# A graph network on one core: TensorE works on the row fetch one chunk further ahead, with the buffers still double

## The chip, the cores and the metric

The kernel runs on one core of a Trainium2 chip. The metric is device time in microseconds, measured without a profiler: the kernel before takes 26865.84 us (median of 3 runs, 26846.94 to 26884.09). A profiled execution of the same program takes longer, and this matters here.

## The reference

Four graph layers follow one another over the same graph of 12,500 nodes and 412,500 directed edges (source `src`, destination `dst`, sorted by destination). Each layer normalises `x`, keeps its positive part `h`, and adds the layer's result to `x`. Per edge a message is made from the source node's row `h[src]`, and the messages of one destination are summed:

```
layer 0: msg = h[src] * edge_weight * weight                      (one number per edge)
layer 1: msg = silu(h[src] x edge_attr_8 x W_msg_tp) @ W_msg_lin  (a tensor product)
layer 2: msg = (h[src] @ W_rel[edge_type]) * e                    (a matrix per relation)
layer 3: w = kernel_net(edge_attr_6), a 16x16 matrix per edge;
         four times: h = gelu(mean over edges of h[src] @ w + h @ root_W + root_b)
out = segment_sum(msg, dst)
```

## The kernel before, in words

Six passes run over the edges in the function `edge_pass`: "weighted" (layer 0), "relational" (layer 2), "kernel_net" (first step of layer 3, which also stores the edge matrices) and three times "kernel_kept" (the other steps, which load them again). Layer 1 has a pass of its own, which is not touched. Partition p holds a stretch of the sorted edges. A pass is a loop over `CHUNKS` = 202 chunks of 16 edges per partition, each edge being one column `j`; even chunks use buffer half b = 0 and odd ones b = 1.

Source rows come in two ways. For columns 0 to 11 (all 16 in kernel_net) GpSimd issues one indirect DMA per column (`gather_chunk`, L575) into `got`, a ring of 4 chunks, so GpSimd may be up to four chunks ahead of VectorE; a buffer comes free with `got_used`. The last X = 4 columns of the five passes other than kernel_net are fetched with matmuls, in these steps for each chunk:

- `hot_rows`: a one-hot of each edge's place in the table, 13 tiles in `place_hot`. ScalarE makes tiles 0 to 8 (nine `near` at L940, then one `place_hot` at L945), VectorE tiles 9 to 12 (L1004).
- place sums (`in_place_sums`, L777): 37 matmuls of 128x512 in four quarters (9, 9, 9 and 10), from `place_hot` and the table's three bf16 parts `tparts`, into `in_place`.
- `pick` on VectorE (L1011): keeps in `picked` the table range that holds the row.
- row sums (`in_row_sums`, L786): four small float32 matmuls with `fold` into `in_row`.
- `fetch` on VectorE (L1019): copies `in_row` into `got` beside the gathered rows.

VectorE then makes the message. In the relational pass a chunk has four groups g; TensorE makes a group's matrices in `wmat` (12 matmuls, L830, two buffers), VectorE multiplies (`product`, L1070) and reduces (`reduce`, L1078). The matrices of group g wait in `matrices` for the product two groups before, that is for a free buffer. A scan (L1111) sums within a destination, ScalarE copies the result (L930) and SyncE stores it. In SyncE's `load` stand the loads of indices, places (`place_b`) and ranges (`range_b`), one chunk after another in order.

The order on each engine is written by hand; semaphores alone tie the engines. Before, TensorE in chunk k makes the row sums of k, three quarters of the place sums of k + 1, and the first quarter of k + 2, which waits for `fetch` of k.

Of the kernel before, what the change touches and what calls it, by code (L numbers as in the profile page):

```python
# [29 lines left out]
P = 128  # L30
# [5 lines left out]
C = 16  # L36
# [543 lines left out]
def edge_pass(nc, a, SB, kind, table):  # L580
# [15 lines left out]
    with ExitStack() as ctx:  # L596
# [56 lines left out]
        with phase(nc, *names) as (block, *sems):  # L653
# [9 lines left out]
            def _(sp):  # L663
# [16 lines left out]
                def load(k, r, q, at):  # L680
# [21 lines left out]
                    if X:  # L702

                        sp.wait_ge(S["hot_by_act"], k + 1)
                        sp.wait_ge(S["hot_by_dve"], k + 1)
                        load_places(k + 2, b)

                        if not (first and b == 0):
                            sp.wait_ge(S["picked_made"], k)
                        load_ranges(k + 1, 1 - b)  # L710
# [27 lines left out]
                if X:  # L738
                    load_places(0, 0)
                    load_places(1, 1)  # L740
                    load_ranges(0, 0)
                    load_whole()
                rounds(sp, load)
# [23 lines left out]
            def _(pe):  # L767
                def in_place_sums(k, b, q, first=False):
# [3 lines left out]
                    if q == 0 and not first:  # L772
                        pe.wait_ge(S["fetched"], k - 1)
# [25 lines left out]
                def close_sums():  # L799

                    for h in range(XH):
                        pe.matmul(in_place[1][:, h, :], SB["zero_b"][:, 0:P], SB["zero_b"][:, 0:XC], start=False, stop=True)

                if X:
                    pe.wait_ge(S["parts_made"], 1)
                    for q in range(4):
                        in_place_sums(0, 0, q, first=True)
                    in_place_sums(1, 1, 0, first=True)

                if kind == "weighted":  # L810

                    pe.matmul(hist[:, :], SB["zero_b"][:, 0:P], SB["zero_b"][:, 0:NQ], start=True, stop=False, skip_group_check=True)
                    with pe.Fori(0, TURNS) as i:
                        for b in range(HALVES):
                            for g in range(4):
                                around(i * HALVES + b, b, g)
                            pe.wait_ge(S["hot_made"], i * HALVES + b + 1)
                            for j in range(C):
                                mm = pe.matmul(hist[:, :], ohp[:, b, j, :], ohq[:, b, j, :], start=False, stop=False, skip_group_check=True)
                            mm.then_inc(S["hot_used"], 1)  # L820
                    close_sums()
# [12 lines left out]
                if kind == "relational":  # L834
                    with pe.Fori(0, TURNS) as i:
                        for b in range(HALVES):
                            pe.wait_ge(S["hot_made"], i * HALVES + b + 1)
                            for g in range(GROUPS):
                                matrices(i * HALVES * GROUPS + b * GROUPS + g, g % 2, onehot[:, b, g * GE:(g + 1) * GE],
                                         [SB["wrel"][:, m, :] for m in range(PIECES)])  # L840
                                around(i * HALVES + b, b, g)
                    close_sums()
                    return

                if kind == "kernel_kept":
                    with pe.Fori(0, TURNS) as i:
                        for b in range(HALVES):
                            for g in range(GROUPS):
                                around(i * HALVES + b, b, g)
                    close_sums()  # L850
# [33 lines left out]
            def _(act):  # L884
# [61 lines left out]

                for b in range(HALVES):
                    hot_rows(b, b, 0, True)
                spread_mask(0, 0, True)
                for b in range(HALVES):  # L950
                    spread_mask(b + 1, 1 - b, b == 0)
                    hot_rows(b + 2, b, 1)
                    turn_out(b, b, 0, True)
                with act.Fori(1, TURNS - 1) as i:
                    for b in range(HALVES):
                        spread_mask(i * HALVES + b + 1, 1 - b, False)
                        hot_rows(i * HALVES + b + 2, b, i + 1)
                        turn_out(i * HALVES + b, b, i, False)
                spread_mask(CHUNKS - 1, 1, False)
                hot_rows(CHUNKS, 0, TURNS)  # L960
                turn_out(CHUNKS - 2, 0, TURNS - 1, False)
                hot_rows(CHUNKS + 1, 1, TURNS)
                turn_out(CHUNKS - 1, 1, TURNS - 1, False)
# [4 lines left out]
            def _(dve):  # L968
# [38 lines left out]
                def pick(k, b, turn_no):  # L1007

                    dve.wait_ge(S["in_place_made"], k + 1)
                    dve.wait_ge(range_in[b], turn_no * 16 + 16)  # L1010
                    dve.scalar_tensor_tensor(out=picked[:, :].rearrange("p (h e) -> p h e", h=XH),  # L1011
# [10 lines left out]
                def chunk(k, r, q, at):  # L1022
# [3 lines left out]
                    rows_v = got[:, r, :].rearrange("p (j f) -> p j f", f=W)  # L1026

# [1212 lines left out]
```

## Time and profile before

| what | value |
|---|---|
| time, median of 3 runs | 26865.84 us |
| span of the profiled execution | 31834.1 us |
| busy share of that span: TensorE, VectorE, ScalarE, GpSimd | 66%, 61%, 40%, 63% |
| mean granted TensorE clock, share of 2.4 GHz | 0.781 |

The span runs from the first to the last instruction of the one profiled execution. Its own time as the runs are timed isn't given; the span alone is 4968 us above the median of the runs. So the profile has idle time that the timed runs don't have, and the busy shares above are shares of the longer span.

### The profile page before, as it was taken

The page shows a single profiled execution, that of the slowest core. Times are in us where ns is not written, and L with a number is a line of the kernel's source. Part 1 is how long each engine was busy: PE and PEld are TensorE (multiplying, and loading weights), DVE is VectorE, ACT ScalarE, POOL GpSimd, SP SyncE. Part 2 cuts the span into 40 slices and gives each one's busy share as a digit, 9 for nine tenths or more (in the row PEclk, how much of TensorE's full clock was granted, in tenths as well). Part 3 has the DMA queues.
Part 4 walks back from the last instruction along what each step waited for, and adds up shares of the span by engine and source line. Part 5 has one row for each costly group of instructions (what it writes and reads, how often), then busy time and mean ns, then how long its engine had stood idle before and what let it go on. Part 6 is the DMA issues. An engine that isn't in the chain of part 4 may idle for free. (4 is left out here: it accounts for less than half of the span.)

```text
span 31834.1 us, 357740 instructions
## 1 busy us (share of the span) xinstructions
PE 21003.5 (66%) x95045; PEld 10976.5 (34%) x95045; DVE 19470.8 (61%) x31805; ACT 12595.6 (40%) x14673; POOL 20017.5 (63%) x18077
## 2 busy tenths in 40 slices
PE   4666649999867777756666666566655656465654
PEld 2333326666533333323333333222222222222222
DVE  4444448888756666645555555566665766566665
ACT  4555511111134444431111111455555655455554
POOL 4666657777734444445555555677776777766666
PEclk8777769999877777777777777777777777777777
DMA  1111125555412222212222222444444544444443
GB/s 38 34 33 34 34 59 93 92 92 93 89 42 50 50 49 49 49 44 86 84 86 84 85 84 82 120 138 146 143 127 130 147 140 145 113 136 136 140 135 106
DMA packets 2202951, 2877.61 MB, mean 90 GB/s; under 512 B 962293, under 2 KB 1687075, under 8 KB 2175143
## 3 DMA queue, kind: packets, MB, share of 16 engines
q1 hardware_dynamic: 1369250, 2680.20, 26.7%
q0 software_dynamic: 804512, 169.87, 8.0%
q10 hardware_dynamic: 29088, 26.49, 0.2%
q8 instruction: 29, 0.48, 0.0%
q14 instruction: 72, 0.58, 0.0%
HBM read 2203.20 MB, written 671.60 MB: 90 GB/s over the span
## 5 line engine op out<-in xcount | busy, mean ns | idle before, releaser
L575 POOL DMA_INDIRECT got<-table,idx x15352 | 16035.5, 1045 | 10224.3 <-issue 4522.0
L777 PE MATMUL in_place<-place_hot,tparts 128*128 128x512 bf16 x37600 | 10862.7, 441 | 5734.9 <-issue 2698.7
L777 PEld LDWEIGHTS in_place<-place_hot,tparts 128*128 128x128 bf16 x37600 | 4005.5, 111 | 11806.1 <-issue 7382.3
L940 ACT ACTIVATE near<-place_b,far_lanes 128x512 bf16<-128x512 f16 x9180 | 5713.3, 707 | 61.9 <-DMA place_b<-place_row 61.4
L1078 DVE TENSOR_REDUCE msg<-prod 128x64 f32<-128x1024 f32 x4040 | 4904.5, 1214 | 103.3
L945 ACT ACTIVATE place_hot<-near,one 128x4608 bf16<-128x4608 bf16 x1020 | 4218.3, 4136 | 1004.0 <-remote 810.9
L930 ACT ACTIVATE outb<-run 128x256 f32<-128x256 f32 (+1 forms) x1010 | 739.3, 732 | 8309.1 <-DVEq L1115 6614.4
L1492 POOL DMA_INDIRECT added<-rows,add_idx x2020 | 3318.9, 1643 | 962.2 <-issue 866.7
L1070 DVE TENSOR_TENSOR prod<-w_in,got 128x1024 f32<-128x1024 f32 x2424 | 2909.9, 1220 | 303.7 <-DMA got<-table,idx 176.5
L1535 PE MATMUL acc<-hot,spread 128*128 128x392 bf16 x14544 | 2849.5, 353 | 0.0
L1063 DVE TENSOR_TENSOR wcopy<-wmat,b 128x1024 f32<-128x1024 f32 x808 | 988.3, 1223 | 2445.7 <-remote 2050.1
L1019 DVE COPY got<-in_row 128x64 f32<-128x64 f32 (+1 forms) x1010 | 227.8, 226 | 3214.3 <-remote 3130.4
L830 PE MATMUL wmat<-k,h 128*128 128x256 f32 x6464 | 1928.1, 452 | 392.4 <-ACT h L896 254.4
L865 PE MATMUL h2p<-h,k 128*128 128x512 f32 x1616 | 1091.7, 763 | 1471.1 <-ACT h L890 1237.2
L890 ACT ACTIVATE h<-h1p,b 128x512 f32<-128x512 f32 x808 | 555.0, 687 | 3713.3 <-remote 2189.7
L1070 DVE TENSOR_TENSOR prod<-wmat,got 128x1024 f32<-128x1024 f32 x808 | 980.6, 1223 | 1652.5 <-remote 1288.9
L830 PEld LDWEIGHTS wmat<-k,h 128*128 128x128 f32 x6464 | 1461.8, 231 | 1171.1 <-issue 499.2
L1011 DVE SCALAR_TENSOR_TENSOR picked<-range_b,range_col,in_place 128x512 f32<-128x512 f16 x1015 | 758.3, 747 | 1803.9 <-remote 1274.0
L1535 PEld LDWEIGHTS acc<-hot,spread 128*128 128x128 bf16 x14544 | 1498.8, 106 | 1020.1 <-issue 258.2
L830 PE MATMUL wmat<-wrel,onehot 90*128 90x256 bf16 x9696 | 1542.9, 305 | 393.6 <-issue 375.3
L786 PE MATMUL in_row<-fold,picked 128*128 128x16 f32 x6464 | 862.0, 266 | 1304.6 <-DVE picked L1011 793.1
L786 PEld LDWEIGHTS in_row<-fold,picked 128*128 128x128 f32 x6464 | 891.3, 204 | 1507.3 <-DVE picked L1011 855.1
(253 smaller groups left out, 18740.6 us busy)
## 6 DMA issues: line engine op xcount, KB each, us to landing
w_in<-kept SPq DMA_DIRECT2D x2424, 512.0 KB
kept<-wcopy SPq DMA_DIRECT2D x808, 512.0 KB
got<-table,idx POOLq DMA_INDIRECT x15352
attr<-in_edge_attr SPq DMA_DIRECT2D x202, 1024.0 KB
place_b<-place_row SPq DMA_DIRECT2D x1020, 128.0 KB
range_b<-range_row SPq DMA_DIRECT2D x1015, 128.0 KB
sums<-outb SPq DMA_DIRECT2D x1010, 128.0 KB
rows<-in_src_row SPq DMA_DIRECT2D x202, 640.0 KB
```

The source lines that it names most:

```text
L575: pool.indirect_dma_start(out=dst[:, j * width:(j + 1) * width], out_offset=None, in_=table, in_offset=bass.IndirectOffsetOnAxis(ap=idx[:, ...
L777: mm = pe.matmul(in_place[b][:, h, :], tparts[:, s, t, :], place_hot[:, b, t, h * XC:(h + 1) * XC], start=(t == 0 and s == 0), stop=(t == ...
L786: mm = pe.matmul(in_row[b][:, j * FW:(j + 1) * FW], picked[:, j * P:(j + 1) * P], fold[:, :], start=True, stop=True)
L830: mm = pe.matmul(wmat[s2][:, j * DD:(j + 1) * DD], weights[:, j * P:(j + 1) * P], moving, start=(m == 0), stop=(m == len(moving_parts) - 1))
L865: pe.matmul(h2p[n % 2][:, :], SB["k2"][:, :], h1[:, n % 2, :], start=True, stop=True).then_inc(S["h2_made"], 1)
L940: act.activation(near[:, t, :], place_b[:, b, :], ACT.Abs, bias=SB["far_lanes"][:, t:t + 1]).then_inc(S["near_made"], 1)
L945: act.activation(place_hot[:, b, 0:ACT_HOTS, :], near[:, :, :], ACT.Relu, bias=SB["one"][:, 0:1], scale=-1.0).then_inc(S["hot_by_act"], 1)
L1063: dve.tensor_tensor(wcopy[:, g, :].rearrange("p (j d) -> p j d", j=G), wmat[g % 2][:, :].rearrange("p (j d) -> p j d", j=G), bcast(SB["b3" ...
L1070: dve.tensor_tensor(prod[:, g % 2, :].rearrange("p (j o i) -> p j o i", j=G, o=D), w.rearrange("p (j o i) -> p j o i", j=G, o=D), bcast(ro ...
L1078: c.step(dve.tensor_reduce(msg[:, b, 0:D, g * G:(g + 1) * G].rearrange("p o j -> p j o"), prod[:, g % 2, :].rearrange("p (j o i) -> p j o ...
L1492: pool.indirect_dma_start(out=SB["added"][y], out_offset=bass.IndirectOffsetOnAxis(ap=add_idx[:, b, y:y + 1], axis=0), in_=add_rows[:, b, ...
L1535: mm = pe.matmul(acc[c][:, 0:RCOLS], spread[:, b, j, s, :], hot[:, b, j, c * RCOLS:(c + 1) * RCOLS], start=False, stop=False, skip_group_c ...
```

## The change

In the five passes with X = 4 each step of the fetch stands one chunk earlier against the rest: in chunk k ScalarE and VectorE make the one-hots of k + 3 (before: k + 2), TensorE all four quarters of the place sums of k + 2 and the row sums of k + 1 (before: of k), and VectorE picks k + 1 at the start of chunk k (before: at the end of it). `place_hot`, `in_place` and `in_row` stay double, `picked` single. Place sums wait for `picked_made` where they waited for `fetched`; row sums also wait for `fetched`, and `pick` for `in_row_made`. At the head of a pass TensorE makes the place sums of chunks 0 and 1 in full; at its end nothing is made for chunks that don't exist. kernel_net is unchanged.

```diff
                     if q == 0 and not first:
-                        pe.wait_ge(S["fetched"], k - 1)
+                        pe.wait_ge(S["picked_made"], k - 1)
...
                     pe.wait_ge(S["picked_made"], k + 1)
+
+                    pe.wait_ge(S["fetched"], k)
...
-                def around(k, b, g):
-
-
-                    if g == 1:
-                        in_row_sums(k, b)
-                    if g < 3:
-                        in_place_sums(k + 1, 1 - b, g + 1)
-                    else:
-                        in_place_sums(k + 2, b, 0)
+                def around(k, b, g, at=None):
+
+                    if g == 2 and (at is None or at + 1 < CHUNKS):
+                        in_row_sums(k + 1, 1 - b)
+                    if at is None or at + 2 < CHUNKS:
+                        in_place_sums(k + 2, b, g)
...
                 if X:
                     pe.wait_ge(S["parts_made"], 1)
-                    for q in range(4):
-                        in_place_sums(0, 0, q, first=True)
-                    in_place_sums(1, 1, 0, first=True)
+                    for b in range(HALVES):
+                        for q in range(4):
+                            in_place_sums(b, b, q, first=True)
+                    in_row_sums(0, 0)
...
+                def turn(k, b, i, at):
+                    if at is None or at + 1 < CHUNKS:
+                        spread_mask(k + 1, 1 - b, at == 0)
+                    if at is None or at + 3 < CHUNKS:
+                        hot_rows(k + 3, 1 - b, i + 1 + b)
+                    turn_out(k, b, i, at is not None and at < HALVES)
...
+                    if X and (at is None or at + 1 < CHUNKS):
+
+                        pick(k + 1, 1 - b, i + b)
+                    if X and (at is None or at + 3 < CHUNKS):
+                        hot_rows(k + 3, 1 - b, i + 1 + b)
...
-                    if X:
-
-                        pick(k + 1, 1 - b, i + b)
```

SyncE's `load` follows: in chunk k it loads the places of k + 3 (after the one-hots of k + 1) and the ranges of k + 2 (after the pick of k).

TensorE in the relational pass, before: the prologue and the first chunk of the loop (half 0). `in_place_7512` is half 0, `in_place_7513` half 1.

```order
1091 L777 MATMUL in_place_7512<-place_hot,tparts 128x512 x37
1092 L777 MATMUL in_place_7513<-place_hot,tparts 128x512 x9
1096 L830 MATMUL wmat_7517<-wrel,onehot 128x256 x12
1098 L777 MATMUL in_place_7513<-place_hot,tparts 128x512 x9
1100 L830 MATMUL wmat_7518<-wrel,onehot 128x256 x12
1101 L786 MATMUL in_row_7514<-fold_rel,picked 128x17 x4
1102 L777 MATMUL in_place_7513<-place_hot,tparts 128x512 x9
1104 L830 MATMUL wmat_7517<-wrel,onehot 128x256 x12
1105 L777 MATMUL in_place_7513<-place_hot,tparts 128x512 x10
1107 L830 MATMUL wmat_7518<-wrel,onehot 128x256 x12
1109 L777 MATMUL in_place_7512<-place_hot,tparts 128x512 x9
```

The same place in the changed kernel, where `in_place_7589` is half 0 and `in_place_7590` half 1.

```order
1091 L780 MATMUL in_place_7589<-place_hot,tparts 128x512 x37
1092 L780 MATMUL in_place_7590<-place_hot,tparts 128x512 x37
1093 L791 MATMUL in_row_7591<-fold_rel,picked 128x17 x4
1097 L837 MATMUL wmat_7594<-wrel,onehot 128x256 x12
1099 L780 MATMUL in_place_7589<-place_hot,tparts 128x512 x9
1101 L837 MATMUL wmat_7595<-wrel,onehot 128x256 x12
1102 L780 MATMUL in_place_7589<-place_hot,tparts 128x512 x9
1104 L837 MATMUL wmat_7594<-wrel,onehot 128x256 x12
1106 L791 MATMUL in_row_7592<-fold_rel,picked 128x17 x4
1107 L780 MATMUL in_place_7589<-place_hot,tparts 128x512 x9
1109 L837 MATMUL wmat_7595<-wrel,onehot 128x256 x12
1110 L780 MATMUL in_place_7589<-place_hot,tparts 128x512 x10
```

The prologue has 28 place sums more and the first row sums; in the chunk, the row sums moved from behind the matrices of g = 1 to behind those of g = 2, so that row sums and nine place sums stand between the matrices of g = 2 and of g = 3 where ten place sums stood.

VectorE at the turn from one relational chunk to the next, before:

```order
1292 L1078 TENSOR_REDUCE msg<-prod 128x4x16
1293 L1097 TENSOR_TENSOR msg<-msg,emix 128x256
1295 L1111 SCALAR_TENSOR_TENSOR run<-mask,msg 128x512
1296 L1011 SCALAR_TENSOR_TENSOR picked<-range_b,range_col,in_place_7513 128x512
1297 L1004 TENSOR_SCALAR place_hot<-place_b,lanes 128x512 x4
1298 L1046 TENSOR_TENSOR eprod<-attr,wvec 128x256
```

And in the changed kernel:

```order
1293 L1091 TENSOR_REDUCE msg<-prod 128x4x16
1294 L1110 TENSOR_TENSOR msg<-msg,emix 128x256
1296 L1124 SCALAR_TENSOR_TENSOR run<-mask,msg 128x512
1297 L1022 SCALAR_TENSOR_TENSOR picked<-range_b,range_col,in_place_7589 128x512
1298 L1012 TENSOR_SCALAR place_hot<-place_b,lanes 128x512 x4
1299 L1059 TENSOR_TENSOR eprod<-attr,wvec 128x256
```

The instructions and their order are the same; pick and one-hots are those of one chunk later, as the other buffer half in the pick's row shows.

## Rows read from the trace of the kernel before

**Rows 1.** The page, its first line.

```profile
span 31834.1 us, 357740 instructions
```

**Rows 2.** Groups on GpSimd, one pass each (weighted, kernel_net, first kernel_kept): count, busy, mean.

```profile
L575 POOL DMA_INDIRECT got<-table,idx x2424 | 2366.2, 976 | 1668.2 <-DVEq L1035 814.1 <-issue 678.0 <-DMA idx<-in_src 176.1
L575 POOL DMA_INDIRECT got<-table,idx x3232 | 3220.5, 996 | 2546.5 <-DVEq L1099 1389.6 <-issue 972.8 <-DMA idx<-in_src 184.1
L575 POOL DMA_INDIRECT got<-table,idx x2424 | 2720.6, 1122 | 954.6 <-issue 732.9 <-DVEq L1099 195.1 <-DMA idx<-in_src 26.5
```

**Rows 3.** Waits of GpSimd over the three kernel_kept passes: total, times, longest.

```profile
POOL got L575 <- DVEq L1099: 874.0, 84, 20.7
```

**Rows 4.** Timeline, picks of two neighbouring chunks at the end of the weighted pass.

```profile
4071.68 0.75 DVE L1011 SCALAR_TENSOR_TENSOR picked<-range_b,range_col,in_place 128x512 f32<-128x512 f16 x1 [1.31 <-PE in_place L777]
4082.09 0.75 DVE L1011 SCALAR_TENSOR_TENSOR picked<-range_b,range_col,in_place 128x512 f32<-128x512 f16 x1 [1.38 <-PE in_place L777]
```

**Rows 5.** Timeline, picks of two neighbouring chunks at the end of a kernel_kept pass.

```profile
23749.30 0.75 DVE L1011 SCALAR_TENSOR_TENSOR picked<-range_b,range_col,in_place 128x512 f32<-128x512 f16 x1 [0.30 <-issue]
23762.50 0.75 DVE L1011 SCALAR_TENSOR_TENSOR picked<-range_b,range_col,in_place 128x512 f32<-128x512 f16 x1 [0.22 <-DVE run L1111]
```

**Rows 6.** Timeline of VectorE over a relational chunk in mid-pass.

```profile
11011.68 0.75 DVE L1011 SCALAR_TENSOR_TENSOR picked<-range_b,range_col,in_place 128x512 f32<-128x512 f16 x1 [0.33 <-DVE run L1111]
...
11026.98 1.22 DVE L1070 TENSOR_TENSOR prod<-wmat,got 128x1024 f32<-128x1024 f32 x1 [7.92 <-remote]
...
11036.34 0.75 DVE L1011 SCALAR_TENSOR_TENSOR picked<-range_b,range_col,in_place 128x512 f32<-128x512 f16 x1 [0.31 <-DVE run L1111]
```

**Rows 7.** Timeline of VectorE over the last relational chunks.

```profile
13954.78 0.75 DVE L1011 SCALAR_TENSOR_TENSOR picked<-range_b,range_col,in_place 128x512 f32<-128x512 f16 x1 [0.31 <-DVE run L1111]
...
13964.34 1.23 DVE L1070 TENSOR_TENSOR prod<-wmat,got 128x1024 f32<-128x1024 f32 x1 [0.15 <-DVE got L1019]
...
13970.66 0.75 DVE L1011 SCALAR_TENSOR_TENSOR picked<-range_b,range_col,in_place 128x512 f32<-128x512 f16 x1 [0.22 <-DVE run L1111]
...
13978.35 1.22 DVE L1070 TENSOR_TENSOR prod<-wmat,got 128x1024 f32<-128x1024 f32 x1 [1.59 <-PE wmat L830]
...
13981.75 1.22 DVE L1070 TENSOR_TENSOR prod<-wmat,got 128x1024 f32<-128x1024 f32 x1 [0.79 <-PE wmat L830]
...
13988.42 0.75 DVE L1011 SCALAR_TENSOR_TENSOR picked<-range_b,range_col,in_place 128x512 f32<-128x512 f16 x1 [0.22 <-DVE run L1111]
```

**Rows 8.** Timeline of TensorE over the same chunks.

```profile
13949.55 2.12 PE L777 MATMUL in_place<-place_hot,tparts 128*128 128x512 bf16 x9 [1.58 <-ACT place_hot L945]
...
13956.07 0.96 PE L786 MATMUL in_row<-fold_rel,picked 128*128 128x17 f32 x8
13956.89 2.10 PE L777 MATMUL in_place<-place_hot,tparts 128*128 128x512 bf16 x9
13958.82 1.48 PE L830 MATMUL wmat<-wrel,onehot 90*128 90x256 bf16 x12
13960.14 2.32 PE L777 MATMUL in_place<-place_hot,tparts 128*128 128x512 bf16 x10
13962.30 1.47 PE L830 MATMUL wmat<-wrel,onehot 90*128 90x256 bf16 x12
13965.82 3.45 PE L777 MATMUL in_place<-place_hot,tparts 128*128 128x512 bf16 x9 [2.04 <-ACT place_hot L945]
```

**Rows 9.** Windows: length, busy time by engine, then granted clock, DMA share, GB/s.

```profile
13949.50:13953.00 3.50, 3.45 (x22) 2.17 (x23) 2.94 (x5) 0.00 (x0) 0.00 (x0) 1.00 0.00 0
13965.80:13969.20 3.40, 3.38 (x10) 1.36 (x11) 3.00 (x5) 0.00 (x0) 0.00 (x0) 0.59 0.00 0
```

**Rows 10.** Timeline of TensorE, kernel_kept in mid-pass, after a gap.

```profile
30012.90 2.31 PE L777 MATMUL in_place<-place_hot,tparts 128*128 128x512 bf16 x5 [3.08 <-issue]
```

**Rows 11.** Timelines at heads of passes: TensorE (relational), GpSimd's fifth chunk (weighted).

```profile
8971.87 12.20 PE L777 MATMUL in_place<-place_hot,tparts 128*128 128x512 bf16 x46 [55.88 <-DVE tparts L1140]
...
259.08 1.03 POOL L575 DMA_INDIRECT got<-table,idx  x1 [7.69 <-DVEq L1035]
```

More of the change, by code:

```diff
@@ L701, in load @@
                             sp.dma_start(w_in[:, b, g, :], SB["kept"][b][bass.ds(i * GROUPS + g, 1), :, :].rearrange("k p w -> (k p) w")).then_inc(w_landed[b * GROUPS + g], 16)
-                    if X:
[L704 to L710, printed above, removed]
+                    if X and (at is None or at + 3 < CHUNKS):
+                        sp.wait_ge(S["hot_by_act"], k + 2)
+                        sp.wait_ge(S["hot_by_dve"], k + 2)
+                        load_places(k + 3, 1 - b)
+                        sp.wait_ge(S["picked_made"], k + 1)
+                        load_ranges(k + 2, b)
                     if kind == "kernel_net" and (at is None or at >= 1):
@@ L804, in _, with whole_turns @@
+                def whole_turns(body):
+                    with pe.Fori(0, TURNS - 1) as i:
+                        for b in range(HALVES):
+                            body(i * HALVES + b, b, None)
+                    for b in range(HALVES):
+                        body(CHUNKS - HALVES + b, b, CHUNKS - HALVES + b)
                 if X:
                     pe.wait_ge(S["parts_made"], 1)
-                    for q in range(4):
-                        in_place_sums(0, 0, q, first=True)
-                    in_place_sums(1, 1, 0, first=True)
+                    for b in range(HALVES):
+                        for q in range(4):
+                            in_place_sums(b, b, q, first=True)
+                    in_row_sums(0, 0)
@@ L810, in _ @@
                 if kind == "weighted":
                     pe.matmul(hist[:, :], SB["zero_b"][:, 0:P], SB["zero_b"][:, 0:NQ], start=True, stop=False, skip_group_check=True)
[L813 to L820, printed above, removed]
@@ L821, in _, with weighted_chunk @@
-                    close_sums()
+                    def weighted_chunk(k, b, at):
+                        for g in range(4):
+                            around(k, b, g, at)
+                        pe.wait_ge(S["hot_made"], k + 1)
+                        for j in range(C):
+                            mm = pe.matmul(hist[:, :], ohp[:, b, j, :], ohq[:, b, j, :], start=False, stop=False, skip_group_check=True)
+                        mm.then_inc(S["hot_used"], 1)
+                    whole_turns(weighted_chunk)
@@ L834, in _, with relational_chunk, kept_chunk @@
                 if kind == "relational":
[L835 to L842, printed above, removed]
+                    def relational_chunk(k, b, at):
+                        pe.wait_ge(S["hot_made"], k + 1)
+                        for g in range(GROUPS):
+                            matrices(k * GROUPS + g, g % 2, onehot[:, b, g * GE:(g + 1) * GE],
+                                     [SB["wrel"][:, m, :] for m in range(PIECES)])
+                            around(k, b, g, at)
+                    whole_turns(relational_chunk)
                     return
                 if kind == "kernel_kept":
[L846 to L850, printed above, removed]
+                    def kept_chunk(k, b, at):
+                        for g in range(GROUPS):
+                            around(k, b, g, at)
+                    whole_turns(kept_chunk)
                     return
@@ L1005, in hot_rows, with pick @@
                     ins.then_inc(S["hot_by_dve"], 1)
-                def pick(k, b, turn_no):
+                def pick(k, b, turn_no, first=False):
                     dve.wait_ge(S["in_place_made"], k + 1)
                     dve.wait_ge(range_in[b], turn_no * 16 + 16)
+                    if not first:
+                        dve.wait_ge(S["in_row_made"], k)
                     dve.scalar_tensor_tensor(out=picked[:, :].rearrange("p (h e) -> p h e", h=XH),
@@ L1146, in _ @@
                     split_table()
-                    pick(0, 0, 0)
+                    dve.sem_inc(S["fetched"], 1)
+                    pick(0, 0, 0, first=True)
+                    hot_rows(2, 0, 1)
                 if kind == "relational":
```

28 lines of the change are left out of this document (10 added, 18 removed).

## The prediction, made before the changed kernel ran

> **What bounds the kernel now.** The profiled execution spans 31834.1 us, the median of the runs is 26865.84, so I ask first which idle time the timed runs can't have. The groups on GpSimd, pass by pass, show the gathers: 0.976 us each in the weighted pass, and 678.0 us of plain issue over 2424 of them, so a chunk of 12 costs GpSimd 12 x (0.976 + 0.28) = 15.07 us [rows 2]. In kernel_net 16 of them cost (3220.5 + 972.8) / 202 = 20.8 us, in the first kernel_kept pass 12 cost (2720.6 + 732.9) / 202 = 17.1 us. Beyond that GpSimd stands still only because VectorE has not given a ring buffer back: 814.1 us in weighted, 1389.6 in kernel_net, 874.0 in the three kernel_kept passes [rows 2, 3].
>
> Now the ends of the passes, when the last gather has been issued. The weighted pass then goes from pick to pick in 4082.09 - 4071.68 = 10.4 us [rows 4]. kernel_kept takes 13.2 us [rows 5]. Both are below GpSimd's 15.07 and 17.1. In the relational pass a mid-pass chunk takes 11036.34 - 11011.68 = 24.66 us, of which 7.92 us is one wait of VectorE that no engine's record explains, which leaves 16.74 [rows 6]; the last two chunks take 13970.66 - 13954.78 = 15.88 and 17.76 us [rows 7], a mean of 16.8.
>
> If the timed runs have none of these waits, they take 31834 - 814 - 1390 - 874 - (24.66 - 16.8) x 202 = 31834 - 814 - 1390 - 874 - 1588 = 27168 us, 1.1% above the median. That is close enough to say: the 4968 us of excess are these stalls, and in the timed runs GpSimd's gathers bound weighted, kernel_net and kernel_kept, and VectorE, now and then held up by TensorE, bounds the relational pass alone [rows 1 to 7].
>
> **The change in weighted and kernel_kept.** It adds no instruction to a steady chunk and leaves GpSimd's gathers as they are. The other engines need 10.4 and 13.2 us against 15.07 and 17.1 [rows 2, 4, 5], so a wait removed or added among them up to about 4 us per chunk is hidden behind the gathers: 0. Were the cover gone, 1 us per chunk would cost 4 x 202 = 808 us. SyncE's loads of places and ranges move by a chunk but wait for events as early as before; the loads of indices, which GpSimd needs, stand behind `picked_made` of the pick at the head of VectorE's chunk instead of at the tail of the one before, which is the same moment. At the end of a pass one pick (0.75 us) [rows 5] falls away, five times, about -4 us; the one-hots and place sums for chunks past the end lay beside waits and bring nothing.
>
> **The head of a pass.** TensorE makes 74 place sums where it made 46 before its first chunk [rows 11], and VectorE's first chunk now starts with a pick that needs the second 37 and the row sums. At 2.10 us for nine [rows 8] 37 sums take 8.6 us, with 0.8 for the row sums 9.4. In weighted and kernel_kept GpSimd has four buffers to fill, 4 x 15.07 = 60 us, before it needs the first back; in the profile it then waited 7.69 us [rows 11], but behind stalls of the kind just set aside. I take 0 for these four and +9 us for the relational pass; all four uncovered would be +38.
>
> **The relational pass, a steady chunk.** This decides. The last chunks show it undisturbed, on TensorE [rows 8]. From a quarter's start to the next work it is 2.0 us for nine sums, 13960.14 - 13958.82 = 1.32 for a group's matrices, 13956.89 - 13956.07 = 0.82 for the row sums, 13962.30 - 13960.14 = 2.16 for ten sums. A chunk of work is 4 x 1.32 + 3 x 1.95 + 2.16 + 0.82 = 14.1 us, VectorE's about 16.4 (between 15.88 and 16.74, [rows 6, 7]), so TensorE idles 2.3 us per chunk in either kernel. Where it idles differs.
>
> Before, it waits for ScalarE's one-hot ahead of the first quarter: 1.58 and 2.04 us [rows 8]. After the gap of 1.58 the granted clock stayed at 1.00 (2.4 GHz) and nine sums took 2.12 us; after 2.04 it was 0.59 over the stretch, that is 1.2 GHz for most of it, and they took 3.45 [rows 8, 9]. That slow quarter came back as two waits of VectorE, 1.59 and 0.79 us, and a chunk 17.76 - 15.88 = 1.9 us longer [rows 7]. At VectorE's mid-pass pace there is more room; I take 1.2 us, in half of the chunks: 0.6 us per chunk.
>
> In the changed kernel this gate goes: the one-hots are a chunk earlier, and no place sum waits for `fetch`. TensorE then runs ahead until `matrices` of g = 2, which needs the buffer that the product of g = 0 frees in the same chunk. Its whole idle time, 2.3 us (2.6 at VectorE's 16.74), gathers there in one gap. What is queued behind it, matrices g = 2 (1.32), row sums (0.82), nine sums (1.93), matrices g = 3 (1.48), is 5.55 us. Before, ten sums stood there alone, 5.0 us. In the last chunks VectorE came to the product of g = 3 at 13964.34, and the matrices of g = 2 began at 13958.82, 5.52 us ahead [rows 7, 8]. So the new chain has no slack: with the clock up it is late by 0 to 0.1 us, and with it down it is late by what the clock costs. Nine sums cost 1.3 more in the row above; a chain of 5.5 us of which 3 us of normal work run at half speed costs up to 2, I take 1.5. How often: 1.58 did not lose the clock, 2.04 did, 3.08 did in kernel_kept, where five sums then took 2.31 us [rows 10]. For 2.3 to 2.6 us I take three in four, a choice between these rows. So after: 0.1 + 0.75 x 1.5 = 1.2 us per chunk, against 0.6 before: +0.6, times 202 = +121 us. Both ends: if the clock never falls after the change, 0.1 - 0.6 = -0.5, or -101 us; if it falls in every chunk and costs 2, and before it cost 0.3, 1.8 us or +364 us.
>
> The Trainium skill, page "TensorE: Matmul & The Clock Gate", section "A second HAM failure mode: psum-queue depth-cycling", says that short idle gaps between groups of matmuls can make the clock swing to and fro, and that the cost lies in the drops and recoveries between bursts. By it both kernels pay, and the one with the longer single gap more; the trace's last relational chunks agree, with 3.45 against 2.12 us.
>
> **Sum.** -4 + 9 + 121 = +126 us. On the profile's own execution that is 31834 + 126 = 31960 if its stalls stayed as they are, which I don't expect of a profile so far from the timed runs; on their median it is 26866 + 126 = 26992 us.
>
> **Rivals.** (a) *No change that can be told.* All waits in four of the five passes are hidden, and in the relational pass the two clock costs cancel within 0.25 us per chunk: between 26812 and 26920. For it: both kernels idle 2.3 us per chunk, and the price and odds of either gap are each from one or two rows. (b) *Faster.* The gate at ScalarE's one-hot is gone, the clock mostly holds, and the relational pass falls to VectorE's own pace: -101 us, or 26765; it decides for this if fewer than one gap in three costs the clock. It could be more if some of the profile's stalls on the fetch (a third of 814 us) were in the timed runs too: then 26500. Against that stands the sum above, which leaves no such time over. The Trainium skill, page "Perfetto Trace Analysis", section "Optimization Strategy", advises to find the gap's cause and make that dependency start sooner, which is what the change does with the one-hots; in this trace the gap is not on VectorE, which is the busiest there. (c) *The change moves nothing in the relational pass either*, because `in_row_made` and `picked_made` tie TensorE to the same chunk: this ends as (a), within it.
>
> **How the numbers follow.** A difference below 0.2% (54 us) can't be told from none here. Slower by the new gap: 0.46. Same, (a) and (c): 0.33. Faster, (b): 0.21. The likeliest case alone runs from +60 to +364: 26925 to 27230. The range down to 26765 and up to 27210 takes in (a) and most of (b).
>
> **What the profile of the changed kernel would show.** In the last relational chunks of TensorE: no gap ahead of a first quarter released by `place_hot`, one gap of 2 to 3 us ahead of the third group's `wmat` released by VectorE's `prod`, and nine sums or twelve matrices at twice their time behind it; on VectorE a wait of 1 to 2 us ahead of the fourth product, released by `wmat`. In weighted and kernel_kept: gathers at 1.25 us start to start, as now. I am wrong if the fourth product never waits, if the gap splits in two, or if kernel_kept's pace in the timed runs is not set by the gathers.

## The result, and the profile after

The changed kernel takes 27372.81 us (median of 4 runs, 27359.41 to 27382.86), the kernel before beside it 26871.5 (4 runs, 26846.94 to 26884.09): ratio 1.0187 [1.0175, 1.02], 501 us slower. A second set of runs (e14) gave 1.0174 [1.0157, 1.0191]. The direction was forecast, the size was not: 27372.81 lies above the range's end of 27210. One of the ten runs of experiment e3 took 48025.56 us, at a granted clock of 0.445, and its ratio leaves that run out.

The page of the changed kernel, its span, the engines' busy times and the granted clock in 40 slices:

```profile
span 27357.6 us, 358670 instructions
...
PE 20225.3 (74%) x94810; PEld 11025.3 (40%) x94810; DVE 19475.5 (71%) x31780; ACT 12562.9 (46%) x14623; POOL 19882.6 (73%) x18077
...
PEclk9988779999988888879999987888878888788887
```

The span is now 27357.6 us, the time of the timed runs. The first profile of before spans 4968 us more than its runs [rows 1], so the two can't be laid on each other. A later profile of the kernel before (experiment e15) has no such stalls, 26792.1 us, and serves from here on. Each pass, from its first gather to its last, in us:

| kernel | weighted | relational | kernel_net | kernel_kept, three |
|---|---|---|---|---|
| before (e15) | 3121 | 3370 | 4085 | 3423, 3390, 3410 |
| changed | 3104 | 3881 | 4087 | 3450, 3385, 3462 |

The relational pass is 3881 - 3370 = 511 us longer, which is the loss: the spans differ by 27357.6 - 26792.1 = 566 us, of which 74 stand in kernel_kept, whose scatter is that large (below), and a second profile of the changed kernel (e14), taken beside e15, has 3880 us too. Per chunk, pick to pick, it is 19.27 against 16.80 us, 2.47 x 202 = 499 us.

The waits of GpSimd's gathers for VectorE over the whole execution say the same from the other side (waiting engine and line, releaser: total, times, longest). Changed:

```profile
POOL got L575 <- DVEq L1108: 851.1, 195, 5.5
```

Before, without stalls (e15):

```profile
POOL got L575 <- DVEq L1095: 321.1, 187, 2.1
```

The 814.1 and 1389.6 us that GpSimd waited for a ring buffer in weighted and kernel_net, and the 874.0 in kernel_kept [rows 2, 3], are gone in both. What is left on VectorE stands in the relational pass, and it grew by 851.1 - 321.1 = 530 us. In the other passes VectorE holds no gather up, at either depth.

Why VectorE is late there is seen on two engines. Waits of the changed kernel in the relational pass:

```profile
DVE prod L1083 <- PE wmat L837: 540.4, 201, 3.4
PE wmat L837 <- DVE prod L1083: 470.3, 200, 4.8
```

And of before (e15) in the same pass:

```profile
PE in_place L777 <- ACT place_hot L945: 307.6, 193, 2.3
PE wmat L830 <- DVE prod L1070: 56.6, 141, 0.6
DVE prod L1070 <- PE wmat L830: 25.1, 61, 1.9
```

Before, TensorE idles 307.6 / 193 = 1.6 us ahead of the first quarter, for ScalarE's one-hot, as in [rows 8]. After, that wait is gone, and 470.3 / 200 = 2.35 us stand in one gap ahead of the matrices of g = 2, in every chunk; VectorE then waits 540.4 / 201 = 2.7 us for the matrices of g = 3, where before it waited 25.1 us in all. Two chunks of the changed kernel, TensorE (start, duration, work, the idle time before and its releaser):

```profile
10007.99 1.49 PE L837 MATMUL wmat<-wrel,onehot 90*128 90x256 bf16 x12 [2.29 <-DVE prod L1083]
10009.32 1.12 PE L791 MATMUL in_row<-fold_rel,picked 128*128 128x17 f32 x8
10010.28 3.62 PE L780 MATMUL in_place<-place_hot,tparts 128*128 128x512 bf16 x9
10013.74 1.48 PE L837 MATMUL wmat<-wrel,onehot 90*128 90x256 bf16 x12
...
10026.07 1.85 PE L837 MATMUL wmat<-wrel,onehot 90*128 90x256 bf16 x12 [2.19 <-DVE prod L1083]
10027.72 1.72 PE L791 MATMUL in_row<-fold_rel,picked 128*128 128x17 f32 x8
10029.28 4.00 PE L780 MATMUL in_place<-place_hot,tparts 128*128 128x512 bf16 x9
10033.08 1.86 PE L837 MATMUL wmat<-wrel,onehot 90*128 90x256 bf16 x12
```

VectorE in the same chunks, picks and the fourth product:

```profile
10003.68 0.75 DVE L1022 SCALAR_TENSOR_TENSOR picked<-range_b,range_col,in_place 128x512 f32<-128x512 f16 x1 [0.33 <-DVE run L1124]
...
10015.25 1.22 DVE L1083 TENSOR_TENSOR prod<-wmat,got 128x1024 f32<-128x1024 f32 x1 [1.65 <-PE wmat L837]
...
10021.87 0.75 DVE L1022 SCALAR_TENSOR_TENSOR picked<-range_b,range_col,in_place 128x512 f32<-128x512 f16 x1 [0.33 <-DVE run L1124]
...
10034.98 1.22 DVE L1083 TENSOR_TENSOR prod<-wmat,got 128x1024 f32<-128x1024 f32 x1 [3.21 <-PE wmat L837]
...
10042.09 0.75 DVE L1022 SCALAR_TENSOR_TENSOR picked<-range_b,range_col,in_place 128x512 f32<-128x512 f16 x1 [0.81 <-DVE run L1124]
```

The same nine sums that take 2.10 us at 2.4 GHz [rows 8] take 3.62 and 4.00 behind the gap, and the chunks last 18.19 and 20.22 us where the wait is 1.65 and 3.21. Windows of the changed kernel, columns as in [rows 9]: the whole pass, the two chunks' chains, and the work behind the second.

```profile
8179.00:12052.00 3873.00, 3406.00 (x18669) 2052.16 (x18667) 3044.01 (x4206) 2237.58 (x2400) 2325.54 (x2401) 0.85 0.25 63
...
10007.99:10015.23 7.24, 7.24 (x42) 4.66 (x43) 5.44 (x6) 6.62 (x6) 5.55 (x6) 0.76 0.09 14
10026.07:10034.96 8.89, 8.89 (x42) 5.71 (x43) 5.44 (x6) 6.82 (x6) 6.79 (x7) 0.62 0.10 14
10034.96:10044.00 9.04, 8.65 (x52) 4.87 (x50) 7.62 (x13) 2.63 (x4) 3.42 (x5) 1.00 0.27 77
```

The chain from the matrices of g = 2 to those of g = 3 takes 7.24 us at a granted clock of 0.76 in the one chunk and 8.89 us at 0.62 in the other, where 5.55 were worked out at 1.00. By these figures 8.89 x (1 - 0.62) x 2 = 6.8 us of the second chain ran at 1.2 GHz and did 3.4 us of normal work, which is what the chain is longer by; in the first it is 3.5 and 1.7 us. These are the only two kinds of chunk: in 199 of the pass's 201 the clock falls behind the gap, and the fourth product waits 3.2 to 3.4 us in 132 chunks and 1.4 to 1.8 in 68. The clock is back at 1.00 by the end of the chain, and falls again in the next chunk.

### The profile page after: what moved, and what is told of

It reads as the page before. It is cut to its first block and busy times, and to the rows that moved or that the text cites. A ratio compares the mean times of both kernels' runs of the same rounds, so it can differ in the third digit from the quotient of the medians.

```text
span 27357.6 us, 358670 instructions
## 1 busy us (share of the span) xinstructions
PE 20225.3 (74%) x94810; PEld 11025.3 (40%) x94810; DVE 19475.5 (71%) x31780; ACT 12562.9 (46%) x14623; POOL 19882.6 (73%) x18077
## 5 line engine op out<-in xcount | busy, mean ns | idle before, releaser
L780 PE MATMUL in_place<-place_hot,tparts 128*128 128x512 bf16 x37370 | 10369.6, 440 | 2517.7 <-ACT place_hot L952 1952.4
L780 PEld LDWEIGHTS in_place<-place_hot,tparts 128*128 128x128 bf16 x37370 | 4101.0, 113 | 8094.3 <-issue 3649.2
L791 PE MATMUL in_row<-fold,picked 128*128 128x16 f32 x6464 | 1066.4, 300 | 1728.9 <-DVE picked L1022 1727.8
L837 PE MATMUL wmat<-k,h 128*128 128x256 f32 x6464 | 1784.4, 429 | 681.2 <-DVE wcopy L1076 674.7
L837 PEld LDWEIGHTS wmat<-k,h 128*128 128x128 f32 x6464 | 1389.9, 218 | 1292.4 <-issue 922.5
L791 PEld LDWEIGHTS in_row<-fold,picked 128*128 128x128 f32 x6464 | 1000.6, 235 | 2092.8 <-DVE picked L1022 2081.0
L837 PE MATMUL wmat<-wrel,onehot 90*128 90x256 bf16 x9696 | 1305.4, 288 | 473.7 <-DVE prod L1083 473.7
L1012 DVE TENSOR_SCALAR place_hot<-place_b,lanes 128x512 bf16<-128x512 f16 x4060 | 1343.5, 390 | 16.9 <-DMA place_b<-place_row 16.9
L837 PEld LDWEIGHTS wmat<-wrel,onehot 90*128 90x128 bf16 x9696 | 985.6, 103 | 900.5 <-DVE prod L1083 572.2
```

Of the source, the lines that this page charges most:

```text
L780: mm = pe.matmul(in_place[b][:, h, :], tparts[:, s, t, :], place_hot[:, b, t, h * XC:(h + 1) * XC], start=(t == 0 and s == 0), stop=(t == ...
L837: mm = pe.matmul(wmat[s2][:, j * DD:(j + 1) * DD], weights[:, j * P:(j + 1) * P], moving, start=(m == 0), stop=(m == len(moving_parts) - 1))
L1012: ins = dve.tensor_scalar(place_hot[:, b, t, :], place_b[:, b, :], SB["lanes"][:, t:t + 1], None, ALU.is_equal)
```

## The experiments

**Theory:** the loss needs two things together: a gap of 2.3 us behind which the clock falls to 1.2 GHz, and there a chain without slack that ends in the fourth product. **Rival 1:** the new order alone is late, whatever the clock does. **Rival 2:** the loss, or part of it, comes from the depth in weighted and kernel_kept.

Each ratio is to the kernel before, run beside it on the same chip. "Wait" is VectorE's for the matrices in the relational pass.

### Depth by pass: e1, e5, e6, e7

A list at the head of the file names the kinds of pass that get the deeper order; the others keep the one of before.

```diff
+DEEP = ("weighted", "kernel_kept")     # e1, e7; e5: kernel_kept alone; e6: weighted alone
...
+    deep = kind in DEEP
...
-                        pe.wait_ge(S["picked_made"], k - 1)
+                        pe.wait_ge(S["picked_made"] if deep else S["fetched"], k - 1)
```

> Weighted and kernel_kept as changed, relational as before. Theory A (the whole loss is TensorE's single idle gap in the relational pass, ahead of the matrices of g = 2, with a chain behind it that has no slack): the time of the kernel before, 26870 within 50 us, and the relational pass at 16.8 us per chunk in the profile. Rival B (the deeper fetch costs in all five passes): a time between, 27000 us or more.

> Only the three kernel_kept passes as changed, weighted and relational as before. e1 was 0.57% faster than the kernel before, which theory A did not say (its passes should be bound by GpSimd's gathers either way). C1 (the gain is in kernel_kept, where three passes and 606 chunks stand): 0.4 to 0.6% faster than before, 26730 to 26790 us. C2 (it is in weighted): the time of before within 0.15%. C3 (it is no gain at all but the scatter of the kernel_kept passes from run to run, whose mean gather is 1.07 to 1.13 us in the profiles): within 0.3% of before, in no fixed relation to e1.

> Only the weighted pass as changed. C1: the time of before within 0.15%. C2: 0.4 to 0.6% faster. C3: within 0.3%.

> The kernel of e1 once more, with more runs. C1 or C2: again 0.4 to 0.7% faster than before. C3: nearer to 1, 0.1 to 0.3%.

| kernel | us | ratio | weighted | relational | kernel_kept, three together |
|---|---|---|---|---|---|
| e1 | 26752.73 | 0.9943 [0.9926, 0.996] | 3108 | 3371 | 10328 |
| e7 (the same) | 26720.46 | 0.9944 [0.9931, 0.9957] | 3104 | 3371 | 10163 |
| e5 | 26844.44 | 0.9978 [0.9964, 0.9991] | 3119 | 3368 | 10219 |
| e6 | 26998.65 | 1.0039 [1.0026, 1.0052] | 3104 | 3369 | 10438 |
| before (e15) | 26802.36 | 0.9996 [0.9986, 1.0006] | 3121 | 3370 | 10223 |

With the relational pass as before, the loss is gone and 0.56% is gained, twice, where the expectation had the time of before. Rival 2 falls: with both kinds of pass deep there is no loss. Depth takes 11 to 17 us off weighted (3104 to 3108 against 3119 and 3121). But the parts don't add up: kernel_kept alone gains 0.22%, weighted alone loses 0.39%, both together gain 0.56%; none of C1 to C3 had all three. The loss of e6 stands in kernel_kept, whose code is that of before there: 10438 against 10223 us. So kernel_kept's pace moves by 2% between programs with the same code in that pass, and by 1.6% between e1 and e7, which are one program (e1's profiled execution, 26914.9 us, was the slowest of its five). So 0.2 to 0.5% in the total can't be put down to depth in it. The pace goes with how many of the three passes' 7272 gathers take over 1.2 us: 1409 in e7, 1592 in e1, 1663 in e6 (it is not all of it: e15 has 1326, and is no faster than e7). Why they do is seen below, where gathers meet products; why one execution has more of them than another stays open.

### Fill the gap: e2, and half of it: e13

Ten matmuls of 128x384, about 1.8 us, stand ahead of the matrices of g = 2. They multiply zeros into columns of `in_row`'s bank that nothing reads.

```diff
                         for g in range(GROUPS):
+                            if g == 2:
+                                for n in range(FILL):    # e2: 10, e13: 5
+                                    pe.matmul(in_row_whole[1 - b][:, 128:512], SB["zero_b"][:, 0:P], SB["zero_b"][:, 0:384], ...)
                             matrices(...)
                             around(k, b, g, at)
```

> The changed kernel with 10 matmuls of 384 columns more per relational chunk, ahead of the matrices of g = 2; their result (a spare part of a PSUM bank) is read by nothing. Theory A1 (the gap lets the clock fall to 1.2 GHz and the chain behind it runs slowly): TensorE does 1.6 us more per chunk and the kernel is still faster than the changed one: the wait ahead of the fourth product falls from 2.7 us to under 0.5, relational pass at 16.7 to 17.2 us per chunk, time 26850 to 26970 us. Rival A2 (the chain is too long at any clock, or TensorE lacks time): the wait stays or grows, 27370 us or more.

> The kernel of e10. Theory A1: faster than the changed kernel (e14) by 1 to 1.8%, between e2 and it: relational pass 17.0 to 18.2 us per chunk. Otherwise level with it.

e2 takes 26861.79 us, 0.9997 [0.9986, 1.0008]; e13 27005.4, 1.0063 [1.004, 1.0086]. Windows over the relational pass, first of e2:

```profile
8196.00:11614.00 3418.00, 3211.74 (x20278) 2026.25 (x20677) 3044.25 (x4206) 2237.34 (x2400) 2331.45 (x2402) 0.98 0.29 72
```

then of e13:

```profile
8190.00:11600.00 3410.00, 3104.64 (x18575) 1915.82 (x18574) 2875.35 (x3974) 2108.59 (x2264) 2207.81 (x2279) 0.92 0.28 68
```

TensorE, in e2, around the gap:

```profile
10015.78 1.79 PE L849 MATMUL in_row<-zero_b 128*128 128x384 bf16 x10
10018.49 1.49 PE L839 MATMUL wmat<-wrel,onehot 90*128 90x256 bf16 x12 [0.93 <-DVE prod L1088]
```

The idle gap is 0.93 us, the clock of the pass 0.98 instead of 0.85, VectorE's wait for matrices 60.1 us in the pass instead of 540.4, and a chunk 17.01 us instead of 19.27. The chain behind the gap is untouched: matmuls of zeros buy 2.26 us per chunk. (e2's profiled execution, 27012.51 us, was the slowest of its ten, so 17.01 is rather too high.) Half the filling leaves gaps of 1.6 us, a clock of 0.92 and 17.98 us. Within e13 the two kinds of chunk stand side by side, with the same instructions: the 107 in which the clock fell take 19.18 us on the mean, the 93 in which it held 16.69. So it is the clock that costs, and rival 1 falls. The expectation for e10, the same kernel, had the clock kept in more than half of the chunks, and just missed that.

### Filler behind the gap: e12

The same ten matmuls behind the matrices of g = 2, between them and `around`.

> The kernel of e9. Theory A1 as before: slower than the changed kernel (e14) by 320 to 650 us, 1.2 to 2.4%. If the place of the extra work doesn't matter: as fast as e2, level with the kernel before.

e12 takes 27226.63 us, 1.0158 [1.0139, 1.0176], and 19.20 us per relational chunk: no more than the changed kernel run beside it (27265.83, 1.0174, and 19.27). The cost that the expectation gave did not come. TensorE and VectorE of e12:

```profile
10019.45 1.48 PE L839 MATMUL wmat<-wrel,onehot 90*128 90x256 bf16 x12 [2.17 <-DVE prod L1088]
10020.77 1.79 PE L851 MATMUL in_row<-zero_b 128*128 128x384 bf16 x10
10022.40 0.96 PE L793 MATMUL in_row<-fold_rel,picked 128*128 128x17 f32 x8
10023.21 2.10 PE L782 MATMUL in_place<-place_hot,tparts 128*128 128x512 bf16 x9
10025.15 1.48 PE L839 MATMUL wmat<-wrel,onehot 90*128 90x256 bf16 x12
...
10026.66 1.22 DVE L1088 TENSOR_TENSOR prod<-wmat,got 128x1024 f32<-128x1024 f32 x1 [1.52 <-PE wmat L839]
```

The gap stays (2.17 us here). In this chunk the whole chain runs at full clock, is 10026.66 - 10019.45 = 7.2 us long, and VectorE waits 1.52 us for it: 7.2 less that wait is 5.7, so a chain of 5.55 has 0.2 us of slack, about none, as forecast. Over the pass the clock is 0.94 instead of 0.85. It fell in 127 of 201 chunks, where the fourth product waits 3.2 us or so; in 72 it held, and the wait is 1.5 or 1.6. So every chunk pays 1.6 us for the extra work, and the clock costs as much again in two of three, where it cost 2.5 on the mean without that work: the sum stays as it was. Why the clock falls less behind the same gap is not explained. e12 against e2 shows that it is the place of the matmuls that helps, not their number.

### Shorten the chain: e3

```diff
+                        group(0); around(k, b, 0, at)
+                        group(1); around(k, b, 1, at)
+                        group(2); group(3)
+                        around(k, b, 2, at); around(k, b, 3, at)
```

> The changed kernel with the matrices of g = 3 right behind those of g = 2, row sums and quarter 2 after both. The gap stays and the clock falls as before, but the chain from the gap to the last matrices is 2.8 us instead of 5.5. Theory A (chain without slack): wait ahead of the fourth product near 0, relational pass 16.4 to 16.9 us per chunk, 26790 to 26900 us, although the granted clock in the pass stays where it was. If the slow clock hurts by TensorE's total time and not by this chain: 27100 us or more.

e3 takes 26867.15 us, 0.9993 [0.9982, 1.0004], 16.95 us per chunk. TensorE and VectorE of e3:

```profile
10005.45 4.67 PE L837 MATMUL wmat<-wrel,onehot 90*128 90x256 bf16 x24 [2.36 <-DVE prod L1091]
10009.91 1.73 PE L791 MATMUL in_row<-fold_rel,picked 128*128 128x17 f32 x8
10011.30 1.23 DVE L1091 TENSOR_TENSOR prod<-wmat,got 128x1024 f32<-128x1024 f32 x1 [0.15 <-DVE got L1038]
10011.48 4.00 PE L780 MATMUL in_place<-place_hot,tparts 128*128 128x512 bf16 x9
```

The gap is there (2.36 us) and the clock falls: 24 matrices take 4.67 us where they take 2.79 at full clock (e4, below). But nothing that VectorE wants soon stands behind them, and the fourth product starts with the 0.15 us of an unhindered one. In the whole pass VectorE waits 27.5 us for matrices, none of it at a fourth product. The clock did not stay where it was, as the expectation had it: the pass has 0.91 instead of 0.85, and the clock fell in 65 of 200 chunks. Those take 16.96 us on the mean, the 135 others 17.00. What is left above before's 16.80 is no matter of matrices; picks, which waited 10.8 us for place sums in before, wait 47.2 here. A lost clock costs nothing without the chain; a chain without slack costs nothing with the clock (e2). The theory needs both, and has both.

### Split the gap: e4, e8

```diff
+                        group(0); around(k, b, 0, at)
+                        group(1); around(k, b, 1, at)
+                        around(k, b, 2, at)
+                        group(2); group(3)
+                        around(k, b, 3, at)
```

> The changed kernel with row sums and quarter 2 ahead of the matrices of g = 2, and the matrices of g = 3 right behind them. The idle time then stands partly ahead of the row sums (they wait for the pick) and partly ahead of g = 2. Theory A: as e3, 26790 to 26900 us, relational pass 16.4 to 16.9 us per chunk, and a higher granted clock than e3 since the gap is split. If the pick gates it more: up to 27000 us.

> The kernel of e4 once more beside e7. In the profiles both have 16.8 us per relational chunk and the same other passes, so by C1 or C2 they should be equal within 0.1%, both 0.3 to 0.6% faster than before; e4 at 0.26% and e1 at 0.57% would then be two samples of one value.

e4 takes 26813.68 us, 0.9974 [0.9964, 0.9983], e8 (the same kernel) 26838.16, 0.9983 [0.9971, 0.9994]. Waits of e4 in the relational pass:

```profile
PE in_row L791 <- DVE picked L1030: 227.6, 198, 1.5
PE in_place L780 <- ACT place_hot L960: 85.1, 168, 0.9
PE wmat L837 <- DVE prod L1091: 68.9, 170, 0.9
...
DVE prod L1091 <- PE wmat L837: 3.3, 2, 2.9
```

and TensorE in one chunk:

```profile
10016.79 1.06 PE L791 MATMUL in_row<-fold_rel,picked 128*128 128x17 f32 x8 [1.50 <-DVE picked L1030]
...
10020.13 2.79 PE L837 MATMUL wmat<-wrel,onehot 90*128 90x256 bf16 x24 [0.32 <-DVE prod L1091]
```

The idle time now lies in three gaps of 227.6 / 198 = 1.15, 0.5 and 0.4 us. The clock is 0.98 and a chunk takes 16.75 us. That is VectorE's own pace, 0.05 below before's 16.80: in this pass the change, with all its waits mended, has nothing more to win. e8 was expected 0.3 to 0.6% below before and within 0.1% of e7; it is 0.17% below before and 0.4% above e7, and most of that stands in kernel_kept (10253 against 10163 us).

### On a stalled chip: e9, e10, e11

e9 is the kernel of e12, e10 that of e13, e11 that of before.

> The same 10 extra matmuls as in e2, but behind the matrices of g = 2, inside the chain from the gap to the matrices of g = 3. If it is the gap that counts (theory A1), the gap stays at 2.3 us or so, the clock falls as in the changed kernel, and the extra work lies on VectorE's path: 1.6 to 3.2 us per chunk, 320 to 650 us slower than the changed kernel, 27700 to 28020 us. If any extra work kept the clock up (the place not mattering), it would be as fast as e2, 26860 us.

> e2 with 5 instead of 10 extra matmuls: 0.8 us of the gap filled, a gap of about 1.5 us left. Theory A1, by the gaps of 1.58 (clock kept) and 2.04 us (clock lost) in the kernel before: the clock is kept in more than half of the chunks, relational pass 17.0 to 18.2 us per chunk, 26880 to 27130 us. If the gain of e2 came otherwise: 27370 us.

> The kernel before once more, for a profile that may lack the stalls of the first. Theory: gathers 1.25 us start to start in weighted without waits (15.4 us per chunk), kernel_kept 16.8 to 17.3 us per chunk, relational 16.8 us per chunk, span within 1% of 26870 us. If the stalls belong to this program under the profiler, they come again and the span is near 31800 us.

On the chip that these ran on, the kernel before took 31872.84 us in the runs without a profiler as well, and e11's span is 31858.2. e9 gave 1.0426 [1.0399, 1.0453], e10 1.0306 [1.0283, 1.0329]. Their loss is not in the relational pass, which takes 4904 us in e9 and 4490 in e10 against 4972 in e11; the three kernel_kept passes, deep in both, take 12283 and 12286 against 11145. So on this chip, under its stalls, the deeper order did cost there; why was not tried. Nothing of the theory can be read from these runs, and both kernels were run again on another chip, as e12 and e13. What the runs do settle is a step of the prediction (below). TensorE in e11:

```profile
12012.59 1.03 PE L777 MATMUL in_place<-place_hot,tparts 128*128 128x512 bf16 x4
12014.14 0.38 PE L777 MATMUL in_place<-place_hot,tparts 128*128 128x512 bf16 x1 [0.52 <-issue]
12015.53 0.38 PE L777 MATMUL in_place<-place_hot,tparts 128*128 128x512 bf16 x1 [1.02 <-issue]
12016.24 1.07 PE L777 MATMUL in_place<-place_hot,tparts 128*128 128x512 bf16 x3 [0.34 <-issue]
```

In stretches single matmuls come 0.7 to 1.4 us apart, with no semaphore behind it. The cause was not tried.

### Both kernels once more: e14, e15

> The changed kernel beside the others: 1.9% slower than before, within 0.2%, wherever the kernel before takes 26870 us. Where that takes 31870 us (stalls), theory A says nothing of the ratio.

> The kernel before, for its profile without the stalls. By the parts of e1, e5 and e6: relational 16.8 us per chunk (pass 3370 us), weighted 3119 us, kernel_net 4095 us, the three kernel_kept passes together 10300 us, which is 135 us above e1's second profile (10163) and 138 below e6 (10438), though e6 has the same code in them. If the deeper fetch gained in kernel_kept, before and e6 would agree.

e14 took 27265.83 us, 1.0174 [1.0157, 1.0191], with 19.27 us per relational chunk; e15 26802.36, 0.9996 [0.9986, 1.0006], with 16.80. Both came as expected but for e15's kernel_kept passes, 10223 us instead of 10300. Window over e15's relational pass, to be read beside the changed kernel's 0.85:

```profile
8190.00:11500.00 3310.00, 2939.54 (x18342) 1797.28 (x18341) 2997.40 (x4128) 2197.63 (x2365) 2322.49 (x2382) 0.97 0.29 73
```

## Why the prediction was right in direction and wrong in size

**The four other passes: right.** "0" for them holds: weighted -17 us, kernel_net +2, kernel_kept 10297 against 10223, inside the scatter of that pass. GpSimd never waits for VectorE there. Head (+9) and tail (-4) of a pass are below what can be read.

**Where TensorE's idle time goes: right.** No gap for `place_hot`, one gap of 2.35 us, released by `prod`, ahead of the matrices of g = 2, and behind it a chain with no slack (shown by e12) whose end holds up the fourth product.

**What the clock costs after: this step failed.** The prediction put it as "0.1 + 0.75 x 1.5 = 1.2 us per chunk". Measured is a wait of 540.4 / 201 = 2.69 us in 201 of 202 chunks, 2.5 above an unhindered product's 0.15. Both factors were too small. "Three in four" was nearly one in one: the clock fell in 199 of 201 chunks. The price is the larger miss, and an error of the working itself: it let "3 us of normal work run at half speed" and gave that "up to 2", took 1.5, though 3 us of work at half speed last 6 and cost 3, in a chain that it had just found to be without slack. The work was judged rightly: in the trace 3.4 us of it ran slowly in 132 chunks and 1.7 in 67, and each cost its own length. The median wait is 3.22 us, more than the "costs up to 2" of the upper end, which is why the range missed too. With 3 us in place of 2 that end is 0.1 + 3 - 0.3 = 2.8 us per chunk, or +566, and would have held the result.

**What the clock costs before: too high.** It was put at "0.6 us per chunk", for gaps of 1.58 and 2.04 us of which the second lost the clock [rows 8, 9]. In the profile without stalls those gaps are 1.6 us on the mean, the clock is 0.97, and VectorE waits 25.1 us in the whole pass, 0.12 per chunk. Of the two rows, the first was the usual case: the clock fell in 54 of 201 chunks, not in half, and these are no longer than the others (16.65 us against 16.82), so nothing of the 1.2 us per fall is left either. With measured terms the sum is (2.5 - 0.1) x 202 = 485 us against 501.

The Trainium skill, page "TensorE: Matmul & The Clock Gate", section "A second HAM failure mode: psum-queue depth-cycling", puts the cost into drops and recoveries between bursts. The trace agrees on the swing, 0.62 in the chain and 1.00 behind it; the cost it shows in the chain's own matmuls, 8.89 us for 5.55.

**The stalls: right in use, wrong in cause.** The prediction took the profile's extra 4968 us for "idle time that the timed runs don't have", and budgeted 27168 us without it. The profiles without stalls bear the budget out: the waits set aside are gone, and e15's chunks take 15.5 us in weighted, 16.8 in relational, 20.2 in kernel_net and 16.9 in kernel_kept, where it had 15.07, 16.8, 20.8 and 17.1. But it laid the gap between profile and times to the profiled execution. e11 and its runs show the same stalls on one chip with no profiler running. That the first profile came from such a chip fits its span (31834.1 us beside e11's 31858.2) but is not shown.

**Rivals.** (a) and (c) needed the two clock costs to cancel; they differ by 2.4 us. (b), the clock mostly holds, gets nothing from the changed kernel. Once the clock does hold (e2, e4), 2.26 and 2.5 us per chunk come back, but the pass is then no more than level with before, 0.05 us per chunk below it in e4; the 0.5 that (b) promised were never there, since the clock cost before so little.

## What to carry to other kernels

Before a wait is moved, add up TensorE's idle time in the loop: it doesn't vanish, and if the new order gathers it in one place, ask which chain stands behind that place and what slack it has at half the clock (2.3 us of gap ahead of a 5.55 us chain cost 2.5 us, 202 times). Where there is no slack, work at half the clock costs its own length again, and a price below that needs a reason. Such a gap is mended by filling it, by splitting it, or by putting first behind it what the other engine wants first; all three gave the 500 us back. And a profile that is far from the timed runs gives the order of events, but no odds: how often a gap loses the clock has to be read from an execution that runs at the timed pace.

## What the runs showed of the hardware

**A gather meets a product.** GpSimd and VectorE in kernel_kept, in e4:

```profile
24014.29 1.23 DVE L1091 TENSOR_TENSOR prod<-w_in,got 128x1024 f32<-128x1024 f32 x1
24014.36 1.98 POOL L575 DMA_INDIRECT got<-table,idx  x1 [0.30 <-issue]
24015.43 1.21 DVE L1099 TENSOR_REDUCE msg<-prod 128x64 f32<-128x1024 f32 x1
24016.64 0.94 POOL L575 DMA_INDIRECT got<-table,idx  x1 [0.30 <-issue]
```

A gather takes 0.94 us, also under a reduce. The one that is issued just behind the start of a float32 product of two operands in SBUF lasts 1.98: the reduce behind the product starts at 24015.43, and the gather ends 0.91 later, as if it had only begun about then. In e4's first kernel_kept pass 590 gathers start under such a product and 528 of them take over 1.2 us; of 803 that start under a reduce none does, and of 601 that start under a relational product, whose matrices lie in PSUM, none either. Each product of kernel_kept can catch one, and most do; in kernel_net, where the product's operands lie in SBUF too, only 50 gathers of the pass are that long, since most that meet a product start just before its end. That fits the means of 1122 and 996 ns [rows 2], and a pass's pace hangs on how the two engines meet. The Trainium skill, page "SBUF — State Buffer", section "🔬 SBUF: two separate sides", tells of a lock on ports shared by VectorE and GpSimd that is held for a whole instruction; the trace agrees with 1.98 against 0.94 us.

**The clock's swing.** Gaps of 1.6 us once per 16.8 us left the mean clock at 0.97 in before, but gaps of 1.6 us left in e13 by five fillers went with 0.92; e12's gaps of 2.3 us went with 0.94, the changed kernel's with 0.85. The length of the gap alone doesn't set it: within e13 the chain behind a gap of 1.38 us ran at 0.76, and the next one, behind a gap of 1.80, at 1.00.

**Stalls of one chip.** The same program took 26871.5 us on one chip and 31872.84 on another. Whether that is the chip or its state at the time is not shown.
